# Scattering the tokens into expert pages within the graph network's turns

## What is computed

```
xn = layernorm(x)
x1 = x + gnn(xn, edge sums, u)             # relu(concat @ W1 + b1) @ W2 + b2
       + mix(xn)                           # 4 layers: linear attention + GELU MLP
z  = layernorm(x1)
e  = argmax(z @ router_w.T + router_b)     # one of 32 experts per node
out = x1 + relu(relu(z @ W1[e] + b1[e]) @ W2[e] + b2[e])
```

## Time and profile before

| | |
|---|---|
| median of 3 runs | 2868.31 us (2865.25 to 2874.70) |
| the profiled execution | 2884.98 us, span 2883.2 us |
| busy: PE / DVE / ACT / POOL | 91% / 74% / 55% / 61% |
| mean granted TensorE clock | 0.956 of full |
| software DMA queue (indirect) | 57600 packets, 7.3% of 16 engines |

### The profile page before, as it was taken

How to read it: one execution, slowest core, us unless ns; L and a number is a source line. 1 busy time by engine, 2 the same in 40 slices (tenths; PEclk the granted TensorE clock), 3 DMA queues, 4 the chain that set the end, 5 groups by cost and what they waited for, 6 DMA issues and landing times.

```text
span 2883.2 us, 57776 instructions
## 1 busy us (share of the span) xinstructions
PE 2631.6 (91%) x19546; PEld 2462.9 (85%) x19546; DVE 2143.3 (74%) x4892; ACT 1581.4 (55%) x3080; POOL 1756.9 (61%) x1614
## 2 busy tenths in 40 slices
PE   5889999999989999998999999899999998993497
PEld 3667899999989999997999999799899998993365
DVE  8988677777767777776777777788888886894055
ACT  0545476666636666664666666444444445671165
POOL 2045587777778777777877776555555553224566
PEclk7999999999999999999999999999999998996699
DMA  6022322222242232224222222343333322201343
GB/s 127 29 49 55 96 64 68 64 58 61 51 116 60 61 69 59 64 45 118 60 64 64 65 59 51 94 120 89 86 89 87 93 75 57 62 26 39 83 116 94
DMA packets 255570, 207.99 MB, mean 72 GB/s; under 512 B 165506, under 2 KB 194387, under 8 KB 255278
## 3 DMA queue, kind: packets, MB, share of 16 engines
q1 hardware_dynamic: 197678, 162.55, 21.8%
q0 software_dynamic: 57600, 41.75, 7.3%
HBM read 136.93 MB, written 70.16 MB: 72 GB/s over the span
## 4 chain that ended last, share of the span: by engine, by line
PE 59%; DVE 15%; POOL 11%; issue 9%; ACT 2%; DVEq 1%; DMA 1%; SPq 0%; ACTq 0%; POOLq 0%; another core or an unknown queue 0%
PE bank L399 54%; POOL edges_sorted L787 7%; PE bank L1918 4%; DVE hidh_lo L1394 3%; POOL tokens_sorted L853 2%; DVE xh L1358 2%; DVE scr L1268 1%; DVE oh L1591 1%; DVEq L1570 1%; PE bank L2381 1%; POOL ehl L803 1%; DVE bn L1349 1%; POOL r L765 1%; DMA queries<-qn 1%; DVE res L1366 1%
## 5 line engine op out<-in xcount | busy, mean ns | idle before, releaser
L787 POOL DMA_INDIRECT edges_sorted<-staging,pos_i x850 | 1075.7, 1265 | 246.4 <-issue 229.8
L910 ACT ACTIVATE hid<-bank,b1p 128x250 f32<-128x250 f32 x800 | 331.5, 466 | 319.3 <-PE bank L399 286.3
L399 PE MATMUL bank<-w_hi,hidh_hi 128*125 128x256 f32 x1600 | 472.2, 295 | 23.1 <-DVE hidh_lo L1394 22.9
L399 PE MATMUL bank<-h_hi,w_hi 128*128 128x250 f32 x1600 | 479.1, 299 | 3.7 <-DVE h_lo L1378 3.4
L399 PE MATMUL bank<-w_hi,hidh_lo 128*125 128x256 f32 x1600 | 453.7, 284 | 0.0
L1394 DVE TENSOR_TENSOR hidh_lo<-hid,hidh_hi 128x500 fp32r<-128x500 f32 x400 | 319.7, 800 | 178.6 <-ACT hidh_hi L916 145.7
L399 PE MATMUL bank<-w_lo,hidh_hi 128*125 128x256 f32 x1600 | 452.2, 283 | 0.0
L399 PE MATMUL bank<-h_hi,w_lo 128*128 128x250 f32 x1600 | 448.5, 280 | 0.0
L399 PE MATMUL bank<-h_lo,w_hi 128*128 128x250 f32 x1600 | 445.0, 278 | 0.0
L399 PEld LDWEIGHTS bank<-w_hi,hidh_hi 128*125 128x125 f32 x1600 | 300.8, 188 | 32.1 <-DVE hidh_lo L1394 29.3
L399 PEld LDWEIGHTS bank<-h_hi,w_hi 128*128 128x128 f32 x1600 | 303.9, 190 | 8.4 <-DVE h_lo L1378 6.1
(11 more groups left out here) (292 smaller groups left out, 6625.5 us busy)
## 6 DMA issues: line engine op xcount, KB each, us to landing
staging<-edges_sorted SPq DMA_DIRECT2D x103, 260.0 KB
staging<-in_edge_attr SPq DMA_DIRECT2D x50, 531.2 KB
queries<-qn SPq DMA_DIRECT2D x100, 250.0 KB
qin<-queries SPq DMA_DIRECT2D x100, 250.0 KB
edges_sorted<-staging,pos_i POOLq DMA_INDIRECT x850
rows_in<-edges_sorted SPq DMA_DIRECT2D x50, 260.0 KB
yin<-tokens_sorted SPq DMA_DIRECT2D x81, 127.0 KB
raw<-in_L_mix_W SPq DMA_DIRECT2D x8, 1024.0 KB, 5.6
```

Source lines behind the costliest of these rows:

```text
L399: return nc.tensor.matmul(o, left, right, start=start, stop=stop, skip_group_check=True)
L787: nc.gpsimd.indirect_dma_start(out=edges_sorted, out_offset=bass.IndirectOffsetOnAxis(ap=pos_i[:, i:i + 1], axis=0), in_=stage[:, slot, j, ...
L910: a = nc.scalar.activation(hid[c % 2][:, j, :], chunks(PH[c % 2])[:, j, :], ACT.Gelu, bias=b1p[:, 2 * c + j:2 * c + j + 1])
```

## The change

The change gives each expert whole blocks ("pages") of 128 rows in `tokens_sorted`, 80 pages in all, handed out while the groups are being routed. When a group's tokens have been counted, each expert whose last page doesn't hold them all is given the next free page. So a token's row is known one turn after it is counted, and its group can be scattered at once.

- SP fills all 80 pages in layer 0, turns 0 to 19, four pages a turn by three DMAs: 256 columns with `tri`, the last four with `unused`, whose third column is 4N, an index past the last node. Rows that no token takes are so left out of the output.
- `chosen` becomes bf16, in four buffers. The counting leaves VectorE: TensorE adds ones and triangular matrices times `chosen` into a bank (`rank_tokens`, five products a turn, two turns behind the choice).
- VectorE gets nine instructions a turn for group i-8, laid between those of the other groups: limits, ranks, pages held, fresh pages, a scan, two selections, a product of 2 x 4 x 32 and a sum of 2 x 5 x 32. Its and TensorE's loops have two more turns.
- GpSimd computes the rows (`token_slots`) and scatters the two tiles of group i-9 in its turn i.
- The mask, the position computation, the segment table and SP's read of first rows go. The kinds of the pages are read back from memory: one DMA of 80 x 4 numbers, then a copy on VectorE.
- In the experts, pages of 128 rows replace segments of 125, 80 replace 81, and the comparison of kinds (L1904) goes. The 48 idle products behind the last scatters become 24, placed after the last count and ahead of the wait for the kinds.
- Some small tiles move (`tri16`, `count16`, `row16` into `hid`), and the setup on GpSimd and VectorE has a few small instructions more.

The diff, cut to its core:

```diff
+            def fill_pages(t):
+                rows = tokens_sorted[t * FILL * PAGE:(t + 1) * FILL * PAGE, :].rearrange("(k p) c -> p k c", p=PAGE)
+                for k in range(KC):
+                    sp.dma_start(rows[:, :, k * 128:(k + 1) * 128], tri[:, :].unsqueeze(1).to_broadcast((PAGE, FILL, 128))).then_inc(blank_written, 16)
+                sp.dma_start(rows[:, :, D:YROW], unused[:, :].unsqueeze(1).to_broadcast((PAGE, FILL, YROW - D))).then_inc(blank_written, 16)
...
+                if l == 0 and 0 <= t < FSEGS // FILL:
+                    fill_pages(t)
...
             sp.wait_ge(f_scat, 16 * TILES)
-            sp.wait_ge(r_table, 2)
+            sp.dma_start(page_kind[:, :, :], tokens_sorted.rearrange("(k p) c -> p k c", p=PAGE)[0:1, :, D:YROW]).then_inc(blank_written, 16)
             for n in range(FSEGS):
-                first = sp.value_load(ffirst_i[0:1, n:n + 1], min_val=0, max_val=N - P)
...
+            def token_slots(g):
+                old, new = g % 2, (g + 1) % 2
+                pool.wait_ge(n_placed, g + 1)
+                of_kind = picked[:, g % 2, :, :]
+                rank, late, more = of_kind[:, :, 4], slots[:, 2, :], slots[:, 3, :]
+                for k in range(2):
+                    own_step(nc.gpsimd.tensor_tensor(slots[:, k, :], of_kind[:, :, 2 * k], of_kind[:, :, 2 * k + 1], ALU.subtract))
+                own_step(nc.gpsimd.tensor_tensor(late, rank, of_kind[:, :, 2 * old + 1], ALU.subtract))
+                pool.wait_ge(p_step, own[0])
+                own_step(nc.gpsimd.tensor_scalar(late, late, 0.0, None, ALU.is_ge))
+                own_step(nc.gpsimd.tensor_tensor(more, slots[:, new, :], slots[:, old, :], ALU.subtract))
+                own_step(nc.gpsimd.tensor_tensor(slots[:, 4, :], slots[:, old, :], rank, ALU.add))
+                pool.wait_ge(p_step, own[0])
+                own_step(nc.gpsimd.tensor_tensor(more, more, late, ALU.mult))
+                pool.wait_ge(p_step, own[0])
+                own_step(nc.gpsimd.tensor_tensor(slots[:, 5, :], slots[:, 4, :], more, ALU.add))
+                pool.wait_ge(p_step, own[0])
+                own_step(nc.gpsimd.tensor_copy(fpos_i[:, PAIR * g:PAIR * (g + 1)], slots[:, 5, :]))
+                SLOTTED[g] = own[0]
+                pool.wait_ge(p_step, own[0])
...
+            for i in range(GROUPS + 9):
                 if i < GROUPS:
                     pool.wait_ge(N_IN[i % 2], 16 * (i // 2 + 1))
                     nc.gpsimd.tensor_tensor(pair(res, i), pair(res, i), x_in[i % 2][:, :, :], ALU.add).then_inc(n_x, 1)
...
+                if i >= 9:
+                    token_slots(i - 9)
+                    scatter_tokens(i - 9)
...
             def route_rank(g):
+                dve.wait_ge(n_ranked, g + 1)
+                dve.wait_ge(n_placed, g)
+                step_(nc.vector.tensor_scalar(limits[:, :], PQT[0:P, PAIR * EXP:(PAIR + 1) * EXP], (PAGE - 1) / 2.0, PAGE_RND, ALU.add, ALU.add))
+                step_(nc.vector.tensor_tensor(picks[:, :, 4, :], PQT[0:P, 0:PAIR * EXP].rearrange("p (j e) -> p j e", j=PAIR),
+                                              chosen[g % CHOICES][:, :, :], ALU.mult))
...
+            def route_pages(g):
+                end_old, held_old, end_new, held_new = book_of(g)
+                stepped()
+                nc.vector.tensor_scalar(held_new, limits[:, :], -PAGE_RND, None, ALU.add).then_inc(n_counted, 1)
+                step_(nc.vector.scalar_tensor_tensor(out=fresh[:, :], in0=limits[:, :], scalar=-PAGE_RND, in1=held_old, op0=ALU.add, op1=ALU.subtract))
...
+            def rank_tokens(g):
+                now, last = chosen[g % CHOICES], chosen[(g - 1) % CHOICES]
+                both = "p j e -> p (j e)"
+                pe.wait_ge(n_chosen, g + 1)
+                pe.wait_ge(n_counted, COUNTED + g)
+                if g:
+                    mm(PQT[0:P, 0:PAIR * EXP], rest_r[0:P, 0:P], last[:, :, :].rearrange(both), False, False)
+                    mm(PQT[0:P, 0:EXP], ones_r[0:P, 0:P], last[:, 1, :], False, False)
+                mm(PQT[0:P, 0:PAIR * EXP], tri_r[0:P, 0:P], now[:, :, :].rearrange(both), g == 0, False)
+                mm(PQT[0:P, EXP:(PAIR + 1) * EXP], ones_r[0:P, 0:P], now[:, 0:1, :].to_broadcast((P, PAIR, EXP)), False, False)
+                mm(PQT[0:P, PAIR * EXP:(PAIR + 1) * EXP], ones_r[0:P, 0:P], now[:, 1, :], False, False).then_inc(n_ranked, 1)
...
+            for i in range(2, GROUPS + 8):
                 def live(d):
                     return 0 <= i - d < GROUPS
+                if live(8):
+                    rank_tokens(i - 8)
...
+            for _ in range(IDLE_LOAD):
+                idle_product()
             pe.wait_ge(r_table, 2)
```

More of the change, by code:

```diff
@@ L51 @@
 YROW = D + 4
-FSEGS = TILES + EXP - 1
+PAGE = 128
+PAGE_RND = 8388608.0 * PAGE
+FILL = 4
+CHOICES = 4
+FSEGS = (N + EXP * (PAGE - 1)) // PAGE
 RIN = 6
@@ L320, in build @@
         besti = sb("besti", [P, PAIR, 8], U32)
[L321 to L324, removed]
+        chosen = [sb(f"chosen{i}", [P, PAIR, EXP], BF16) for i in range(CHOICES)]
+        tri_r = sb("tri_r", [128, 128], BF16)
+        ones_r = sb("ones_r", [128, 128], BF16)
+        rest_r = sb("rest_r", [128, 128], BF16)
+        fpos_i = sb("fpos_i", [P, TILES], I32)
+        slots = sb("slots", [P, 6, PAIR])
+        limits = sb("limits", [P, EXP])
+        fresh = sb("fresh", [P, EXP])
+        ends = sb("ends", [P, 2, EXP])
+        book = sb("book", [P, 4, EXP])
+        picks = sb("picks", [P, PAIR, 5, EXP])
+        picked = sb("picked", [P, 2, PAIR, 5])
         cT = both("cT", [128, 3, GT])
@@ L663, in step @@
                     load_queries(l, t + 3)
+                if l == 0 and t == 0:
+                    sp.wait_ge(consts, NCONST)
+                if l == 0 and 0 <= t < FSEGS // FILL:
+                    fill_pages(t)
                 if l == -1 and t == SCATTERS_FROM - 1:
@@ L865, in _ @@
                     in_=orow[n % OUTS][:, :], in_offset=None, bounds_check=N - 1, oob_is_err=False).then_inc(F_OUT[n % OUTS], 16)
-            for slot in range(OUTS):
-                pool.wait_ge(F_OUT[slot], 16 * (FSEGS // OUTS))
+            for i in range(OUTS):
+                pool.wait_ge(F_OUT[i], 16 * len(range(i, FSEGS, OUTS)))
         @block_.scalar
@@ L1814, in route_chosen @@
                 stepped()
[L1815 to L1819, removed]
+                if g >= CHOICES:
+                    dve.wait_ge(n_ranked, g - CHOICES + 2)
+                nc.vector.tensor_tensor(chosen[g % CHOICES][:, :, :], iota_seg[0:P, 0:EXP].unsqueeze(1).to_broadcast((P, PAIR, EXP)),
+                                        pair(res, g, D + 4)[:, :, D + 3:D + 4].to_broadcast((P, PAIR, EXP)), ALU.is_equal).then_inc(n_chosen, 1)
@@ L1822, in route_count @@
                 stepped()
[L1823 to L1829, removed]
-                stepped()
-                step_(nc.vector.tensor_reduce(frank[:, PAIR * g:PAIR * (g + 1)], rank_j[:, :, :], AX, ALU.add))
+                step_(nc.vector.tensor_tensor_scan(ends[:, g % 2, :], ones[0:P, 0:EXP], fresh[:, :], ends[:, (g + 1) % 2, EXP - 1:EXP], ALU.mult, ALU.add))
@@ L1836, in _ @@
             nc.vector.tensor_tensor(g2[1][:, :, :], raw_g2[:, :, :], f32(g2[0][:, :, :]), ALU.subtract).then_inc(gw_lo, 1)
-            for i in range(1, GROUPS + 6):
+            for i in range(1, GROUPS + 8):
                 def live(d):
```

184 lines of the change are left out of this document (92 added, 92 removed).

## The result

The changed kernel takes **2836.85 us** in the median of 4 runs (2836.61 to 2842.52), against 2866.78 for the kernel before in the same comparison (4 runs, 2864.87 to 2874.7): a ratio of 0.9895, 95% interval 0.9872 to 0.9918. It is faster by some 30 us, 1%, where 48 had been forecast. The profiled execution took 2836.78 us, of it 2835.1 span.

The account below looks back on a forecast made before the run. TensorE was taken to bound the graph turns, GpSimd's scatters the stretch behind them. Terms -56.3 + 8.5 + 1.0 - 1.6 = -48.4 us, taken from 2868.31, gave 2820 us; range of 8 in 10: 2804 to 2846.

Parts of the forecast that it names:

- The likeliest case: Whole kernel: the forecast of 2820 us, with graph turns of 9.0 us bounded by TensorE; chance 0.62.
- The second rival: Graph turns: VectorE becomes the bound at 9.9 us a turn, +15.5 us over 17 turns, 2836 us; chance 0.18.
- the old stall of 1.1 us: Graph turns before the change: VectorE's two-element L1790 takes 1.25 us beside GpSimd's L846, against 0.15 without it.
- The step that failed: the stall: Graph turns: GpSimd's later add returns half of VectorE's 1.1 us stall, inside its slack of 0.9 us: 0.
- VectorE's own work: Graph turns: four instructions go and nine come, net +0.8 us a turn with overlap, 8.1 us needed, cost 0.
- TensorE: Graph turns: five bf16 products add 0.5 us a turn over 17 turns, nothing hiding it: +8.5 us.
- The tail: From VectorE's turn 25 to SP's first load of sorted tokens: 63.0 us in place of 119.3, -56.3 us.
- The fills, 0: Layer 0, turns 0 to 19: SP's 60 transfers filling the pages are taken as 0, up to 10 us.
- Kinds by transfer, +1.0: Start of the experts: kinds arrive by a transfer and a VectorE copy, +1.0 us, between 0 and 3.4.
- One segment fewer and the clock, -1.6 and 0 +-5: Experts: 80 segments for 81 save 1.6 us; fewer idle products swap one clock loss for another, 0 +-5.
- The base: Whole kernel: the profiled execution, 2884.98 us, lay 16.7 above the median; the forecast was taken from 2868.31.
- the slower rival: Graph turns: TensorE pauses and loses its clock, +6.6 us a turn, 2932 us if all 17; chance 0.03.

Follow-up runs that it names:

- e3: Changed kernel with a small memset and a wait for it between GpSimd's second scatter and its add, from turn 10 on: 2823.09 us (one run).
- e1: Changed kernel with GpSimd's add waiting, from turn 9 on, until VectorE's residual of the same turn has run: 2815.36 us.
- e5: The kernel of e1 with one more VectorE sum of 384 columns a turn, ahead of `graph_low`: 2822.54 us.
- e4: The kernel of e1 with TensorE's five products of the ranks computed twice more a turn, into spare columns: 2824.78 us.
- e6: Changed kernel with all 50 scatters put behind the last group's slots: 2881.93 us, ratio 1.0052 to the kernel before.
- e7: Changed kernel with the fills of the pages run in layers 0, 1 and 2 in place of layer 0 alone: 2838.83 us.
- b0: The kernel before, unchanged, profiled a second time: 2864.16 us.
- e2: Changed kernel with GpSimd's add moved behind the root, still ahead of slots and scatters: 2825.22 us (one run).

## Why the prediction was right and where it failed

The direction and the range (2804 to 2846) held, and the time was 17 us above the forecast. The likeliest case did not: turns of 9.0 us bounded by TensorE. The second rival came in its place, VectorE as the bound, at 10.5 us a turn where it had 9.9. That rival was given 2836 us, and 2836.85 were measured, by luck in good part: its conditions were instructions that don't overlap and the old stall of 1.1 us on the comparison, and what came was some overlap and a stall of 2.0 on another instruction; the turns were dearer than it said, and the tail was cheaper than forecast.

- **The step that failed: the stall.** "I take it that half of the 1.1 us returns, inside VectorE's slack of 0.9: 0." It was 2.0 us a turn. I had placed the add rightly, across the end of VectorE's turn, and had named the comparison as the one with two SBUF inputs there. I had overlooked `graph_hidden_low(i - 2, 1)`, which also reads two and stands three instructions earlier, beside the second scatter; and I had taken the add's own length for the most that it can cost. e3 and e1 show that the add queued directly behind the scatter holds VectorE from before its own start. In the turns this is the loss: 15 x 2.0 us, and 1.7 in turn 8, make up the 31.6.
- **VectorE's own work** was +1.15 us a turn, not +0.8 (e5: 8.5 against 7.34; turn 24 of the changed kernel, without a stall: 8.49), inside the bounds of 0.8 to 1.5. The nine instructions last 2.34 us together, as forecast; it is the overlap with their neighbours that gave 0.35 in place of 0.7. The slack that was to cover the stall was 0.35 us and not 0.9.
- **TensorE**: 0.28 us for five products (priced by e4), 8.85 us a turn in e1, against 0.5 and 9.0. With the bound on VectorE it cost nothing.
- Together the turns gave +31.6 in place of +8.5 us, 23.1 too little in the sum. The tail gave 1.8 more than forecast and turn 8 came 1.5 earlier, the small terms below were 1.3 too low: -27.3 against -48.4 by the spans. The medians lie 2.6 us further apart than the spans, and the kernel before measured 1.5 below the 2868.31 that I started from; so 2836.85 is 17 over 2820.
- **The tail**: -58.1 against -56.3. A group took 4.96 us, not 5.6, since waits on GpSimd's own results cost less than I gave them. Against that stands a pause of 3.85 us ahead of the 40th scatter, put down to issue; the kernel before has one of 3.67 us ahead of its 40th and e6 one of 3.69 ahead of its 40th. I had not counted it per group, and so it was missing in my 9 x 5.6. SP went on 2.6 us after the last scatter instead of 3.9.
- **The fills, 0**: right (e7, and the window above).
- **Kinds by transfer, +1.0**: not felt. From SP's first load to ScalarE's first page 3.1 us pass, before 3.4.
- **One segment fewer and the clock, -1.6 and 0 +-5**: together +0.7. The granted clock of the first 12.8 us in the experts was 0.70, where b0, with its 48 idle products beside the start, had 1.00. 0.3 of 12.8 us is 3.8 us at most, enough to eat the segment saved; that it was this was not tried.
- **The base.** I measured the sum against a profiled execution that was 16.7 us above the median and asked only how far apart the two were. b0 shows where: in the experts, 168.0 us against 147.2. TensorE was busy there for 13.2 us more (148.15 against 134.99), with stretches at half clock such as the earlier trace rows, and paused for 7.6 more. I had read the earlier trace rows as the kernel's habit ("Before, it fell to that anyway"); it belonged to that execution, and b0 does not have it. It did no harm here because the forecast was taken from the median.
- **Clock in the turns**: 1.00 in the window above although TensorE paused for 17 us in it, at most 1.1 us at a time; the slower rival had nothing to stand on.

The rule that I had weighed (the Trainium skill, SBUF — State Buffer, "Who interferes with whom": two SBUF inputs on VectorE and a GpSimd instruction that reads SBUF keep each other out for the whole instruction) agrees with each stall that lies beside the add and ends with it: e2's 1.27, e3's 1.21, e6's 0.85 us. By it L1822 would have lost at most what the add lasts, 1.3 us; the measured 2.0 us, most of them beside a scatter and before the add, are more, and there the measurement decides.

## What to carry to other kernels

An instruction moved to another place on its queue must be laid beside every instruction that the other engine has within its reach, with the operands of each, not only beside the one last on the list. Where two engines keep each other out, give the disturbing instruction a wait that puts it beside work that it hardly holds, here the statistics with one SBUF input (0.2 us lost): one wait on a semaphore that was there already was worth 25 us. And "the new work fits under the bound" is worth what the slack is worth: with 0.35 us left, any longer stall on the second engine makes it the bound of the whole loop.

## What the runs showed of the hardware

- An indirect DMA on GpSimd alone did not disturb VectorE's two-input instruction (0.67 us in e1 and e3, 0.68 in e2). A GpSimd add with two SBUF inputs right behind it (0.02 us from end to start) held that instruction for 2.0 us, from its start inside the scatter until about the add's end; in one turn a two-input instruction that had started 0.09 us before the scatter was not held, and a cast of two columns behind it was, at 2.12 us for 0.15. A small memset and a wait between the two were enough to end it. Behind an ordinary instruction (e2's root) the queued add held nothing before it began. What in the engine does this, no run here tells, nor whether it is the add's wait or its reads that stand in the way.
- The 40th indirect scatter of the tokens has 3.65 to 3.85 us of idle time before it, where the other scatters that follow directly on one have 0.30, in the kernel before, in the changed one and in every experiment, wherever it lies in time. The cause stays open.
- A product of 32 to 64 bf16 columns, with its weight load, costs TensorE 0.055 us in a full stream (e4: 8.8 us for 160).
- The same kernel differed by 20.8 us between two profiles, all of it in its last stretch (168.0 and 147.2 us, at mean granted clocks of 0.91 and 0.98), while the turns before it agreed to 0.1 us (b0).
